# Layer-norm statistics taken by the stages that write the residual, and first loads waited for in groups

## The reference

```python
def _layernorm(x, axis=-1, eps=1e-05):
    m = jnp.mean(x, axis=axis, keepdims=True)
    v = jnp.var(x, axis=axis, keepdims=True)
    return (x - m) / jnp.sqrt(v + eps)

x = x + stage_i(_layernorm(x), ctx, masks, weights)      # i = 0 .. 11
```

| stage | what it computes |
|---|---|
| L0a, L0x, L0f | log-linear attention with a convolution and 32 heads; causal linear attention to the context; mixture of 8 experts, top 2, with a shared expert |
| L1a, L1x, L1f | softmax attention with distance bias, 16 heads; masked softmax attention to the context; gated MLP on quantised values |
| L2a, L2x, L2f | long convolution of a state space model; single-head masked attention to the context; mixture of 8 experts, top 1 |
| L3a, L3x, L3f | linear attention with rotary embedding and a layer norm of its own; softmax attention to latents; mixture of 8 experts, top 2, with a shared expert |

## Time and profile before

### The profile page before, as it was taken

One profiled execution on the slowest core, in us unless ns is written; L12 is line 12 of the kernel. 1 busy time (PEld: TensorE's weight loads), 2 busy tenths in 40 slices (PEclk: granted clock), 3 DMA queues, 4 the chain that ended last, 5 costly groups with the idle time before them and its releaser, 6 DMA issues. The chain is left out here.

```text
span 3803.9 us, 55022 instructions
## 1 busy us (share of the span) xinstructions
PE 2993.7 (79%) x18517; PEld 2140.6 (56%) x18517; DVE 2362.6 (62%) x5278; ACT 1790.9 (47%) x4259; POOL 698.8 (18%) x817
## 2 busy tenths in 40 slices
PE   4889889998978789377687671596799858888697
PEld 3667666676656567255455331444598435555485
DVE  5766777677566423777677768697511485555423
ACT  4666666766532222477577454312333325556221
POOL 0000000000110232155344200000111002334422
PEclk8999999999989799699899895798799979999898
DMA  3101101110100368100000000000397101000476
GB/s 102 45 26 48 42 29 34 40 45 29 34 18 1 134 220 277 35 1 1 25 9 4 26 1 0 3 0 9 138 344 274 52 25 35 24 24 12 151 257 209
DMA packets 109094, 264.76 MB, mean 70 GB/s; under 512 B 16880, under 2 KB 71408, under 8 KB 103824
## 3 DMA queue, kind: packets, MB, share of 16 engines
q1 hardware_dynamic: 93328, 229.00, 18.0%
q0 software_dynamic: 8688, 23.78, 1.7%
q10 hardware_dynamic: 6800, 8.46, 0.7%
HBM read 213.65 MB, written 47.54 MB: 69 GB/s over the span
## 5 line engine op out<-in xcount | busy, mean ns | idle before, releaser
L2977 POOL TENSOR_TENSOR L0a_sum_sq<-L0a_sum_sq,L0a_sq 128x512 f32<-128x512 f32 x56 | 76.8, 1372 | 967.1 <-ACT L0a_sq L2919 967.1
L1296 POOL TENSOR_TENSOR L3x_p<-L3x_p,L3x_rsum 128x512 f32<-128x512 f32 x128 | 133.0, 1040 | 447.6 <-DVE L3x_rsum L1377 447.6
L3023 DVE SCALAR_TENSOR_TENSOR L0a_xf<-L0a_xc,L0a_conv,L0a_xf 128x256 f32<-128x256 f32 x432 | 191.3, 511 | 30.1 <-ACT L0a_xf L2884 28.8
L2835 ACT ACTIVATE L0a_ex<-bank,L0a_nb 128x128 f32<-128x128 f32 x512 | 144.6, 368 | 97.1 <-PE bank L2766 96.5
L3032 DVE TENSOR_TENSOR L0a_ru<-bank,L0a_um 128x512 f32<-128x512 f32 x128 | 88.0, 688 | 150.9 <-PE bank L2758 146.0
L1358 DVE SCALAR_TENSOR_TENSOR L3x_s<-bank,L3x_bias 128x512 f32<-128x512 f32 x128 | 86.4, 681 | 132.9 <-PE bank L1136 132.9
L2686 PE MATMUL bank<-x_feat,L0a_wx 128*128 128x256 f32 x576 | 152.7, 415 | 18.7 <-DMA L0a_wx<-in_L0a_wx 13.0
L1986 PE MATMUL bank<-L2a_half,L2a_diag 128*128 128x512 f32 x328 | 144.1, 601 | 28.4 <-ACT L2a_diag L1969 28.4
L1296 POOL TENSOR_TENSOR L1x_p<-L1x_p,L1x_rsum 128x512 f32<-128x512 f32 x128 | 132.2, 1040 | 135.6 <-DVE L1x_rsum L1377 135.6
L1300 POOL TENSOR_TENSOR L1a_p<-L1a_p,L1a_rsum 128x128 f32<-128x128 f32 (+1 forms) x256 | 123.0, 506 | 135.0 <-DVE L1a_rsum L1377 133.0
L2686 PEld LDWEIGHTS bank<-x_feat,L0a_wx 128*128 128x128 f32 x576 | 113.5, 205 | 47.0 <-DMA L0a_wx<-in_L0a_wx 13.2
(11 more groups left out here) (731 smaller groups left out, 8217.3 us busy)
## 6 DMA issues: line engine op xcount, KB each, us to landing
L2f_wt<-in_L2f_w SPq DMA_DIRECT2D x23, 2180.0 KB, 9.7
L0f_wt<-in_L0f_w SPq DMA_DIRECT2D x39, 898.0 KB, 6.0
L3f_wt<-in_L3f_w SPq DMA_DIRECT2D x39, 768.0 KB, 5.2
L0a_wx<-in_L0a_wx SPq DMA_DIRECT2D x72, 256.0 KB, 3.2
L0a_wz<-in_L0a_wz SPq DMA_DIRECT2D x32, 512.0 KB, 4.3
context_keys_values<-L2f_zeros ACTq DMA_DIRECT2D x32, 256.0 KB, 5.0
L0f_xs<-rows_by_expert SPq DMA_DIRECT2D x39, 128.5 KB, 3.2
L3f_xs<-rows_by_expert SPq DMA_DIRECT2D x39, 128.5 KB, 2.7
```

The source lines that it names most:

```text
L1296: last = nc.gpsimd.tensor_tensor(both, both, rsum[r % 2][:, i, :].unsqueeze(2).to_broadcast([P, S, NK]), ALU.mult)
L2835: last = a(ex[g % 3][:, j, b * P:(b + 1) * P], bank[:, at:at + P], ACT.Exp, bias=nb[r % 2][:, b, h:h + 1])
L3023: vec.scalar_tensor_tensor(out=xf[q % 4][:, j, :], in0=xc[q % 3][:, j, i:i + T], scalar=conv[:, 2 * p + j, i:i + 1], in1=xf[q % 4][:, j, : ...
```

## The change

Two new buffers in `Core`, `c.stats` and `c.mv`, hold means and variances of the 16 tiles of `c.x` over the whole kernel. A new function fills them for given tiles:

```diff
+        self.stats, self.mv = sb("x_stats", [P, NT, 6]), sb("x_mean_var", [P, NT, 2])
...
+def moments(c, vec, ch, tiles):
+
+    one = lambda a, t: a[:, bass.ts(t, 1), :].rearrange("p a d -> p (a d)")
+    for t in tiles:
+        last = vec.bn_stats(one(c.stats, t), one(c.x, t))
+    ch.link(last)
+    for t in tiles:
+        vec.bn_aggr(one(c.mv, t), one(c.stats, t))
```

`normalise` leaves its own statistics out unless it is told `measured=False`, which n0a and L3x_n are; the other eight read `c.mv`. Its `Sqrt` goes ahead of the copies of `also`:

```diff
-                for t in range(NT):
-                    last = nc.vector.bn_stats(stats[:, t, :], src[:, t, :])
-                last.then_inc(sig("stats"), 1)
...
+                if not measured:
+                    for t in range(NT):
+                        last = nc.vector.bn_stats(stats[:, t, :], src[:, t, :])
...
             @block.scalar
             def _(act):
+                act.wait_ge(sig("var_eps"), 1)
+                nc.scalar.activation(rstd[:, :, 1], rstd[:, :, 0], ACT.Sqrt).then_inc(sig("std"), 1)
                 if also is not None:
...
-                act.wait_ge(sig("var_eps"), 1)
-                nc.scalar.activation(rstd[:, :, 1], rstd[:, :, 0], ACT.Sqrt).then_inc(sig("std"), 1)
```

`routed` reads `c.mv` too, and its loads signal three semaphores (`n_small` is the length of the list ahead of the shared expert's tensors):

```diff
-                for to, come_from in pairs:
-                    sp.dma_start(to, come_from).then_inc(sig("loaded_sp"), 16)
+                for i, (to, come_from) in enumerate(pairs):
+                    sp.dma_start(to, come_from).then_inc(sig("loaded_shared" if i >= n_small else "loaded_small" if i else "loaded_gate"), 16)
...
-                pe.wait_ge(sig("loaded_sp"), 16 * len(pairs))
                 for n in range(NBLK + 1):
...
                     if n:
+                        if n == 1:
+                            pe.wait_ge(sig("loaded_gate"), 16)
...
                 if shared:
+                    pe.wait_ge(sig("loaded_shared"), 16 * (len(pairs) - n_small))
                     rise_shared(0, [0])
...
                     if n < NBLK:
-                        ts = range(4 * n, 4 * n + 4)
-                        for t in ts:
-                            last = v.bn_stats(stats[:, t, :], c.x[:, t, :])
-                        ch.link(last)
-                        for t in ts:
-                            last = v.bn_aggr(mv[:, t, :], stats[:, t, :])
-                        ch.link(last)
-                        v.tensor_scalar_add(rstd[:, 4 * n:4 * n + 4, 0], mv[:, 4 * n:4 * n + 4, 1], 1e-5).then_inc(sig("var_eps"), 1)
+                        v.tensor_scalar_add(rstd[:, 4 * n:4 * n + 4, 0], c.mv[:, 4 * n:4 * n + 4, 1], 1e-5).then_inc(sig("var_eps"), 1)
...
-                dve.wait_ge(sig("loaded_sp"), 16 * len(pairs))
+                dve.wait_ge(sig("loaded_small"), 16 * (n_small - 1))
...
                 for t in range(NT // 2, NT):
                     combine(t)
+                    if tag != "L3f":
+                        moments(c, v, ch, [t - NT // 2, t])
```

Every stage that is followed by one of these takes the statistics after it has added to `c.x`, on VectorE, behind a wait for its own add:

```diff
+                    def measure(r):
+
+                        dve.wait_ge(sig("added"), r + 1)
+                        moments(c, vec, ch, [row_of(r) * TB + t for t in range(TB)])
```

More of the change, by code:

```diff
@@ L169, in transpose_tokens, with normalise @@
     sig.close()
-def normalise(c, tag, src, dst=None, dstT=None, gain=None, shift=None, eps=1e-5, loads=(), also=None):
+def normalise(c, tag, src, dst=None, dstT=None, gain=None, shift=None, eps=1e-5, loads=(), also=None, measured=True):
     nc = c.nc
@@ L1455, in _ @@
                     output(ROWS - 1)
+                    for r in range(max(0, ROWS - 2), ROWS):
+                        measure(r)
             sig.clear()
@@ L1588, in _ @@
                         add(i)
+                        measure(i - 1)
+                    measure(n - 1)
             sig.clear()
@@ L2023, in join, with measure @@
                     last.then_inc(sig("joined"), 1)
+                def measure(q):
+                    dve.wait_ge(sig("added"), 4 + q + 1)
+                    moments(c, vec, ch, range(4 * q, 4 * q + 4))
                 def add(k):
@@ L2030, in add @@
                         vec.tensor_tensor(xs, xs, c.banks[q][:].rearrange("p (a d) -> p a d", a=4), ALU.add).then_inc(sig("added"), 1)
+                        if k and q:
+                            measure(q - 1)
                 for k in range(KD):
@@ L2038, in _ @@
                 add(1)
+                measure(3)
         sig.clear()
@@ L2225, in finish, with measure @@
                     xr = c.x[:, r * TB:(r + 1) * TB, :]
-                    vec.tensor_tensor(xr, xr, res[:], ALU.add)
+                    vec.tensor_tensor(xr, xr, res[:], ALU.add).then_inc(sig("added"), 1)
+                def measure(r):
+                    dve.wait_ge(sig("added"), r + 1)
+                    moments(c, vec, ch, range(r * TB, (r + 1) * TB))
                 for i in range(B + 3):
@@ L2237, in _ @@
                         heads(i - 1)
+                measure(B - 1)
         sig.clear()
@@ L2504, in _ @@
                             add(r - 1)
+                        if gi == 3 and r:
+                            measure(r - 1)
                         if gi == 3 and r + 1 < ROWS:
@@ L3147, in finish, with measure @@
                     xr = c.x[:, r * TB:(r + 1) * TB, :]
-                    vec.tensor_tensor(xr, xr, yacc[:], ALU.add)
+                    vec.tensor_tensor(xr, xr, yacc[:], ALU.add).then_inc(sig("finished"), 1)
+                def measure(r):
+                    dve.wait_ge(sig("finished"), r + 1)
+                    moments(c, vec, ch, range(r * TB, (r + 1) * TB))
                 for s in steps:
@@ L3186, in _ @@
                         finish(rho - 2)
+                    if at == 9 and rho >= 2:
+                        measure(rho - 2)
+                measure(B - 1)
         sig.clear()
@@ L3331, in program, with _ @@
             transpose_tokens(c, "ctxT", c.ctx, c.ctxT)
+            sig = Signals(nc, "measure")
+            with nc.Block() as block:
+                @block.vector
+                def _(dve):
+                    moments(c, nc.vector, Chain(dve, sig("dve_chain")), range(NT))
+            sig.clear()
+            sig.close()
         for n in layers:
```

43 lines of the change are left out of this document (32 added, 11 removed).

## The result

| what | before | changed |
|---|---|---|
| median of 16 runs of each | 3815.35 us | 3804.68 us |
| lowest and highest run | 3806.17, 3825.29 | 3796.68, 3816.81 |
| ratio to before, 95% interval | | 0.9971, 0.9962 to 0.9981 |
| profiled execution, span | 3803.9 | 3810.8 |
| VectorE instructions, busy | 5278, 2362.6 us | 5278, 2372.1 us |

The change is 0.29% faster, 11 us. 17.4 us less were forecast (3795.1 against the median known then, 3812.5). The measured median lies inside the whole range, 3782 to 3815, and 0.7 us above the forecast's own range, 3787 to 3804. VectorE has 5278 instructions in both kernels; they stand in other places.

The account below looks back on a forecast made before the run. No engine carries the whole span; at stage boundaries the statistics sit alone on the path. Gains -61.5, stage ends +35.7 and loops +8.4 sum to -17.4, giving 3795.1 us; own range 3787 to 3804, whole range 3782 to 3815.

Parts of the forecast that it names:

- Six table-load blocks, 5.5 each: L1a_n, L1x_n, n1f, n2a, n2x, n3a: `Sqrt` starts when the table load ends, 5.5 us earlier each, 33.0 in all.
- n3x: Normalisation block without a table load: `Sqrt` starts at 3110.55 instead of 3117.09, a gain of 6.5 us.
- n0x: Block where x's transposes follow the context's directly, with TensorE at the faster clock level: a gain of 3.7 us.
- The expert stages' starts, 18.3: Starts of L0f, L2f and L3f: the choice of experts comes earlier by 8.1, 3.7 and 6.5 us.
- TensorE could start at 3533.5, 8.0 earlier: Start of L3f: first transpose 8.0 us earlier; 4.9 left if its chain takes 20.6, so 6.5 was taken.
- The ends of the stages, 35.7: Behind a stage's last add no work covers the last statistics: a cost of 35.7 us summed over the stages.
- its upper end, 8.4: L2x's loop: sixteen single-tile statistics each lengthen a turn, 8.4 us, against 0.6 if they lie in VectorE's idle third.
- Inside the loops, 8.4: Statistics inside the pipelined loops not hidden by other work: a cost of 8.4 us, bounds 0 and 32.4.
- L0a: ... between 0 and 7 x 0.92 = 6.4, I take 3: L0a's loop, VectorE at 71%: seven pairs cost 3 us, as TensorE is the bound but short of full.
- L3x's "4.4": L3x's loop: six pairs cost 4.4 us, since ScalarE waits for VectorE's maxima and VectorE is the path.
- The rival of exposed loops: Loops hide nothing: every pair comes through, 32.4 instead of 8.4, +24.0 us, 3819.1; chance 0.10.
- Given back later: Expert stages L0f, L2f, L3f lose their 18.3 us to something later that doesn't move; 3813.4 us, chance 0.08.

Follow-up runs that it names:

- e9: Against e5: GpSimd's memset of the zeros in the expert stages waits for VectorE's second addition of eps; ratio to the kernel before 0.9937.
- e11: Against e10: GpSimd's memset of the zeros waits until VectorE has normalised two groups; ratio to the kernel before 0.9919.
- e8: The changed kernel once more, unaltered, one execution for a second profile; span 3794.6 us.
- e2: Changed kernel with five boundaries undone (L0a to n0x, L0x to L0f, L1a to L1x_n, L1x to n1f, L3x to L3f); ratio to before 0.9973.
- e4: Changed kernel with the expert stages' loads waited for all at once, as before, so only the statistics are moved; ratio to before 1.0005.
- e7: Changed kernel with L0a's statistics at step 7 and those of L2x, L2a, L0f and L2f in one batch; one execution, L2x +6.46 us against before.
- e5: Changed kernel with L0a's statistics at step 11 instead of 9 and the boundaries into L1a_n, n2x and L2f undone; ratio to before 0.9935.
- e10: Against e9: softmax-stage statistics taken while the last row is in work wait for the end of the stage; ratio to the kernel before 0.9926.
- e1: Kernel before with only the expert stages' loads waited for in groups by three semaphores, all statistics where they were; ratio to before 0.999.
- e6: Against e5: normalisation blocks that take their own statistics take them in four groups of four tiles; ratio to the kernel before 0.9931.

## Why the prediction was right in sum, and where its steps were off

**Six table-load blocks, 5.5 each: right.** 5.25, 5.74, 5.67 and 5.63 in the first profile and the same within 0.1 in the second; n2x gave 6.4, because that block was longer before (17.51 us, where n2a had 16.66). n3a has no stretch of its own; the first add behind it came 4.4 to 4.6 earlier. n3x 6.7 for 6.5. n0x 4.2 and 5.3 for 3.7, with transposes at the faster level.

**The expert stages' starts, 18.3: right in sum in one profile, 4.8 short in the other, and wrong for L3f.** By the choice of experts L0f gave 10.4 and 7.3 (forecast 8.1), L2f 4.8 and 3.4 (3.7), L3f 2.9 and 2.9 (6.5): 18.1 in one profile, 13.5 in the other. The step that failed is "TensorE could start at 3533.5, 8.0 earlier": it started 6.4 earlier (3.69 behind the stage's start against 10.09). The addition of eps was priced at its 0.17 of before and took 1.77, held by GpSimd's memset. e9 and e11 show that this is what holds it: moved, the memset held the next `tensor_scalar` beside it until its own end, and with none of the first group's beside it L3f's start came to 2.10. The same hold is why L0f's first transpose stands 3.69 us behind the stage's start and not the 3.2 forecast (3.28 in e9). The rest is the chain: it took 20.95 us where before it was 17.5, so 3.5 of the 6.4 were given back; 1.5 had been allowed for. Most of that goes with the clock. Over all profiles and the three expert stages the chain is 17.5 to 19.3 us where one of its stretches of 5 us was granted 0.57 or more, and 20.5 to 22.2 where every stretch shows 0.50.

**The ends of the stages, 35.7: near.** L0f's pairs cost 0.92 each, as priced, L2a 6.7 for 6.8, L1f 0.0 to 0.2 for 1.0. L3a with n3a is +0.2 and +0.5 where -1.1 was expected, so 1.5 more: about 1.0 is missing ahead of the first add, and the pairs cost 5.0 in place of 4.4, nearly all of it in the last rows and the end. L2x was taken at its upper end, 8.4, and cost 9.1 (e8, e2, e4) and 11.7 (the first profile, one turn 2.0 longer); against the batch of e7 (6.5) pieces cost 2.6 more.

**Inside the loops, 8.4: the mis-sized term.** "L0a: ... between 0 and 7 x 0.92 = 6.4, I take 3" was the step: the pairs cost about 1.0 for each of L0a's rows, up to 1.3, and all of it is exposed, because a busy share of 71% says nothing of the place. e5 moved the same instructions by two steps, and most of the cost vanished. L1a's and L1x's pairs show in the last row alone, 0.7 and 0.6 to 2.2 us (e10), and at the end, 1.8 each. That L1a was 3.9 longer is for the most part not theirs, as e2 shows. L3x's "4.4" was too much: against e2, which takes no statistics there, the stage is 4.3 longer, 2.3 of it the end, so the loop paid 2.0. L0x cannot be sized: its rows switch between 21.0, 22.6 and 24.1 us in kernels with and without statistics.

**The rival of exposed loops** was thus true of L0a, in part of L3x and of the last rows of L1a and L1x, and the 24 us that it forecast did not come: with all five loop boundaries undone (e2) the time is the same. **Given back later** was true of TensorE's chain only: in L3f it took 17.5 us before and 20.6 to 22.2 in all kernels but e11, and in e1 it lost all that the earlier start had won. Why the clock rose in one execution and not in the other stays open.

**How much of the sum is luck.** The measured gain is 11 us where 17.4 were forecast. In both profiles L0a, L1a, L3a and L3f came out 1.3 to 5.1 us dearer each than forecast, and n0x, n2x, L1f and L3x 0.5 to 1.6 cheaper each. These errors cancel in part, and that part is luck.

**What is left open.** The span is 6.9 longer in one profile and 9.3 shorter in the other; the timed runs have 11 shorter. The part of the execution (L0x, L2f's stores, the clock at the start of L0f, L1x's first row) was seen and not controlled. What made the store in L2f land so late was not tried.

**A better kernel.** e5 is 0.65% faster than before (0.9919 to 0.9952), against 0.29% for the change (0.9962 to 0.9981): L0a's statistics stand ahead of a wait of VectorE, and the boundaries into L1a_n, n2x and L2f are left alone. e6, e9, e10 and e11 (0.9937 to 0.9919) build on it, and none can be told from it.

## What to carry to other kernels

Work moved under a loop costs what the place costs, not what the engine's busy share suggests: look in the timeline for a wait of the same engine directly behind the new place. Behind a run of serial VectorE work, statistics cost the same as in the block that they came from, and in pieces more (0.55 us for a tile alone, 0.41 in a batch of 16). Where two waits hold the same instruction, take both away and read when it starts: here both together brought the first transposes of the three expert stages 15.9 us forward, where one alone brought 10.5 and the other 1.4. When an instruction moves, look what another engine runs beside it at the new time: GpSimd's memset and its first copies had cost nothing beside `bn_stats`. And where single executions spread by more than the effect, compare the profiles stage by stage and take a second one of the same kernel.

## What the runs showed of the hardware

GpSimd's memset of 128x2056 (1.81 us) holds VectorE's `tensor_scalar` until about 0.15 us behind its own end: 128x4 took 1.76 us beside it and 0.17 alone, 128x256 took 1.60 and 1.90, and 0.41 alone. GpSimd's copy of 128x1024 (1.04 us) held one of 128x256 for 1.05. The `bn_stats` beside the same memset in the kernel before took 1.41 for four, as always, and a reciprocal of 128x4 its 0.18 (e9), so these were not held. The Trainium skill's page "SBUF — State Buffer", section "SBUF: two separate sides", says that GpSimd and VectorE share one port pair, as an exclusive lock that a VectorE operation in a two-port mode waits for. The trace agrees with the hold; whether these `tensor_scalar` ran in such a mode no run shows (in a run of them each further 128x256 takes 0.32 us, near the 0.33 of `bn_stats`).

TensorE's transposes ran at the 2.4 GHz level in n0x (16 in 1.91 us at a granted clock of 1.00, with nothing else on the engine), where the Trainium skill's page "TensorE: Matmul & The Clock Gate", section "Part 4: PE-mode transpose", has the full clock not engage; the trace disagrees. Like work at the start of L0f, 9.76 and 9.75 of 10 us busy, was granted 0.67 in one execution and 0.50 in another: 3 us of difference in the same program.
